# Softmax attention: the maximum subtracted on VectorE instead of GpSimd, two units interleaved

## What is computed

```python
qkv = xn @ Wqkv.T                      # q, k, v, 16 heads each
s = einsum('bhqd,bhkd->bhqk', q, k) * 16 ** -0.5
s = where(causal, s, -inf)
p = softmax(s, axis=-1)                # exp(s - max(s)) / sum
x = x + einsum('bhqk,bhkd->bhqd', p, v).reshape(b, t, 256) @ Wout.T + bout
```

## Time and profile before

| | |
|---|---|
| median of 3 runs | 2348.63 us (2345.78 to 2349.6) |
| the profiled execution: time | 2340.59 us |
| its span, first to last instruction | 2338.8 us |
| granted clock of TensorE, mean | 0.951 |
| busy: PE, PEld, DVE, ACT, POOL | 2115.2, 1578.8, 1472.2, 1112.8, 980.7 us |
| L1133, the subtractions on GpSimd | 64, 68.1 us busy, 1064 ns in the mean |

### The profile page before, as it was taken

The page is one execution under the profiler, slowest core; times in us unless marked ns, Lnnn a source line. Parts: engine busy times, 40 slices in busy tenths (PEclk is TensorE's granted clock), DMA queues, the critical chain, the costliest instruction groups (busy, mean ns, idle before and its releaser), DMA issues. The chain is left out here.

```text
span 2338.8 us, 57804 instructions
## 1 busy us (share of the span) xinstructions
PE 2115.2 (90%) x19590; PEld 1578.8 (68%) x19591; DVE 1472.2 (63%) x4145; ACT 1112.8 (48%) x2509; POOL 980.7 (42%) x1105
## 2 busy tenths in 40 slices
PE   6999999999989998999999999979969898777773
PEld 5888888888779986565566666647758787433331
DVE  5777777777656664784333333327867767777672
ACT  4666666666645442275122222216445555444542
POOL 4444444444300003344566666652123433145554
PEclk9999999999989988999899999989979999899996
DMA  4110010111000003040222222237710000000002
GB/s 137 33 31 30 30 30 30 30 30 30 30 8 10 11 10 111 1 198 18 77 87 85 88 87 85 87 124 279 240 42 11 7 9 7 3 0 1 0 0 72
DMA packets 120510, 128.80 MB, mean 55 GB/s; under 512 B 77537, under 2 KB 95074, under 8 KB 119138
## 3 DMA queue, kind: packets, MB, share of 16 engines
q1 hardware_dynamic: 104994, 87.12, 12.2%
q0 software_dynamic: 13824, 37.77, 5.1%
q10 hardware_dynamic: 1600, 2.72, 0.3%
HBM read 96.11 MB, written 27.26 MB: 53 GB/s over the span
## 5 line engine op out<-in xcount | busy, mean ns | idle before, releaser
L542 ACT ACTIVATE xa_prob<-xa_neg_s,xa_neg_max 128x256 f32<-128x256 f32 x512 | 224.5, 499 | 141.4 <-DVE xa_neg_max L420 141.4
L1904 PE MATMUL ex_ps_h<-moew_w,ex_xT 128*128 x576 | 274.9, 600 | 1.5 <-DVE ex_xT L1952 1.5
L1952 DVE COPY ex_xT<-ex_ps_x 128x256 f32<-128x256 f32 x144 | 61.1, 425 | 249.1 <-PE ex_ps_x L1911 249.1
L420 DVE CUSTOM_DVE_ANT_0 xa_neg_s<-xa_ps_s,xa_mask 128x256 f32<-128x256 f32 x512 | 191.4, 421 | 33.6 <-PE xa_ps_s L607 19.4
L1883 POOL DMA_INDIRECT ex_xg<-xn_rows,moe_in_row x144 | 139.6, 970 | 107.5 <-PE ex_ps_x L1911 98.6
L636 PEld LDWEIGHTS xa_ps_o<-xa_v,xa_probT 128*64 128x64 f32 x4096 | 141.2, 138 | 48.3 <-issue 43.0
L549 ACT ACTIVATE xa_probT<-xa_ps_s 128x512 f32<-128x512 f32 x256 | 152.0, 594 | 43.3 <-PE xa_ps_s L618 42.3
L636 PE MATMUL xa_ps_o<-xa_v,xa_probT 128*64 128x34 f32 x4096 | 170.2, 228 | 0.2 <-ACT xa_probT L549 0.2
L1937 ACT ACTIVATE ex_act_g<-ex_ps_h 128x256 f32<-128x256 f32 x144 | 55.2, 383 | 236.6 <-PE ex_ps_h L1904 236.6
L1888 POOL DMA_INDIRECT expert_outs<-moe_y,moe_out_row x144 | 142.1, 986 | 60.9 <-ACT moe_y L1941 59.1
L618 PE MATMUL xa_ps_s<-g_ident,xa_prob 128*128 128x128 f32 x1024 | 163.8, 283 | 2.7 <-ACT xa_prob L542 2.4
(11 more groups left out here) (319 smaller groups left out, 5090.1 us busy)
## 6 DMA issues: line engine op xcount, KB each, us to landing
xa_ctxT<-in_ctxT_dram SPq DMA_DIRECT2D x32, 512.0 KB, 3.6
xb_ctx_rows<-in_ctx_rows_dram SPq DMA_DIRECT2D x32, 512.0 KB, 3.7
xb_expert_y<-expert_outs SPq DMA_DIRECT2D x32, 512.0 KB, 4.4
moew_w<-in_moe_w_dram SPq DMA_DIRECT2D x8, 1024.0 KB, 11.8
xn_rows<-rs_xn SPq DMA_DIRECT2D x8, 512.0 KB, 2.9
moew_xw<-in_moe_w_dram SPq DMA_DIRECT2D x8, 512.0 KB, 19.7
out_dram<-g_x SPq DMA_DIRECT2D x1, 4096.0 KB, 13.5
g_x<-in_x_dram SPq DMA_DIRECT2D x2, 1536.0 KB, 15.3
```

What stands on the lines that cost most here:

```text
L420: ins = nc.vector.tensor_tensor_reduce(neg_s[:, u % 2, g, :], ps_s[j][:, g * S:(g + 1) * S], mask[:, b, :], -1.0, 3e38, ALU.add, ALU.min, ...
L542: ins = nc.scalar.activation(prob[:, u % 2, i, :], neg_s[:, u % 2, i, :], ACT.Exp, bias=neg_max[:, u % 2, i:i + 1], scale=-1.0)
L1904: mm = nc.tensor.matmul(ps_h[1 - par][:, :], xT[:, 1 - par, k, :], c.w1[:, own, k, :], start=(k == 0), stop=(k == KC - 1))
```

## The change

GpSimd no longer subtracts. VectorE does, in the same form (`less_largest`), and takes the units by twos in a new function, `below_maximum`: mask, maximum, mask of the next, subtract, maximum of the next, subtract of the next. What waited for GpSimd's subtraction before a unit's mask is now one wait ahead of each pair of units, on VectorE's own subtraction. The wait for the exponential two units back goes along with the subtraction. Sizes, buffers and the other engines' programs stay as they are.

```diff
--- before.py
+++ after.py
@@ -1126,13 +1126,6 @@
                 a = s - 2
                 if live(s, NP) and later(s):
                     start.inverse_std(pool, nc, s, par)
-                if live(a, NP):
-                    for j in range(4):
-                        pool.wait_ge(top_ready, 4 * a + j + 1)
-                        wait(pool, exp_ready, 4 * a + j - 1)
-                        nc.gpsimd.tensor_tensor(shifted[:, j % 2, :, :], masked[:, j % 2, :, :],
-                                                top[:, j % 2, :].unsqueeze(2).to_broadcast([P, 8, T]), ALU.subtract)\
-                            .then_inc(shift_ready, 1)
                 if live(s, NP):
                     pool.wait_ge(xn_ready, s + 1)
                     for i in range(2):
@@ -1143,14 +1136,32 @@
 
         @block.vector
         def _(dve):
-            def maximum(a, j):
+            def mask_added(a, j):
                 dve.wait_ge(s_done, 4 * a + j + 1)
-                wait(dve, shift_ready, 4 * a + j - 1)
                 nc.vector.tensor_tensor(masked[:, j % 2, :, :], ps_s[j][:, :].rearrange("p (n t) -> p n t", t=T),
                                         mask[:, :].unsqueeze(1).to_broadcast([P, 8, T]), ALU.add)\
                     .then_inc(masked_ready, 1)
+
+            def largest(a, j):
                 dve.wait_ge(masked_ready, 4 * a + j + 1)
                 nc.vector.tensor_reduce(top[:, j % 2, :], masked[:, j % 2, :, :], AX.X, ALU.max).then_inc(top_ready, 1)
+
+            def less_largest(a, j):
+                dve.wait_ge(top_ready, 4 * a + j + 1)
+                wait(dve, exp_ready, 4 * a + j - 1)
+                nc.vector.tensor_tensor(shifted[:, j % 2, :, :], masked[:, j % 2, :, :],
+                                        top[:, j % 2, :].unsqueeze(2).to_broadcast([P, 8, T]), ALU.subtract)\
+                    .then_inc(shift_ready, 1)
+
+            def below_maximum(a, j):
+                if j == 2:
+                    dve.wait_ge(shift_ready, 4 * a + 2)
+                mask_added(a, j)
+                largest(a, j)
+                mask_added(a, j + 1)
+                less_largest(a, j)
+                largest(a, j + 1)
+                less_largest(a, j + 1)
 
             def normalised_heads(e, i):
                 heads = ps_o[i][:, 0:H * D1].rearrange("p (h d) -> p h d", d=D1)
@@ -1188,15 +1199,14 @@
                                 k2[:, pp, 0, g, :, h2, :], ALU.mult, ALU.subtract)
                     ins.then_inc(k_ready, 1)
                 if live(a, NP):
-                    maximum(a, 0)
-                    maximum(a, 1)
+                    wait(dve, shift_ready, 4 * a)
+                    below_maximum(a, 0)
                 if live(e, NP):
                     dve.wait_ge(pv_done, 4 * e + 4)
                     for i in range(2):
                         normalised_heads(e, i)
                 if live(a, NP):
-                    maximum(a, 2)
-                    maximum(a, 3)
+                    below_maximum(a, 2)
                 if live(s, NP) and later(s):
                     wait(dve, xT_done, s - 1)
                     start.normalise(dve, nc, s, par)
```

## The result

The changed kernel took 2386.68 us in the median of 4 runs (2385.52 to 2391.67), against 2348.05 us (2345.78 to 2349.6) for the kernel before: a ratio of 1.0169, 95% interval 1.0154 to 1.0183. It is slower, as forecast, but by 38.6 us where the forecast had 26.2. Applied to the 2348.63 us from which the forecast started, the ratio gives 2388.3 us, just above the stated range, which ended at 2387. The profiled execution took 2387.38 us.

A forecast was written before the change was run, and what follows sets the result against it. The prediction took a circle of waits as the bound, with VectorE's run closing it. +2.40 and -0.73 us a step gave 21.7 us over thirteen steps, +26.2 with first and last ones: 2374.8 us, range 2366 to 2387.

The forecast's parts named there:

- VectorE's run as the side of the circle that sets the step: Softmax self-attention: VectorE's run from M, a step's first mask addition, to L1205's end grows from 8.58 to 10.25 us.
- +2.40 us for the subtractions: On VectorE, each of two pairs of units per step takes 3.84 us instead of 2.64, 1.20 more.
- -0.73 us for L233: VectorE's normalisation no longer meets GpSimd's last subtraction: 408 ns instead of 1137, in 14 steps.
- Rival 3: L233 stays slow for a reason other than GpSimd's last subtraction: 10.2 us missing, 2385.0 us; chance 0.10.
- The exponentials: First two come as before, TensorE's 1.22 us wait stays; a new wait for the third is hidden by L1205's lateness.
- First and last steps: First softmax step 1.8 us longer, next-to-last 2.1, last between 0 and 1.2, taken as 0.6.
- The sum: First step 1.8, thirteen steps 21.7, next-to-last 2.1 and last 0.6 us: together +26.2 us.
- Rival 4: Longer TensorE standstills lower its clock to 0.85 over the thirteen steps: 19 us more, 2394 us; chance 0.04.
- the forecast's own signs: Among them: TensorE's wait behind L1205 up from 0.65 to about 1.2 us, a new 0.4 for the third exponential.
- Rival 1: The chain through the subtraction to the first exponential sets the step: 22.4 us saved, 2326.2 us; chance 0.04.
- Rival 2: TensorE's own work absorbs the additional 1.67 us per step, no change: 2348.6 us; chance 0.03.

The follow-up runs named there:

- e3: The changed kernel with one idle 128x512 subtraction per step on GpSimd, started after VectorE's fourth subtraction so it lies over L233: 2417.77 us, 1.0289.
- e7: The kernel before with only the fourth unit's subtraction moved to VectorE, GpSimd keeping three: 2351.28 us, 1.0009.
- e1: The changed kernel with seven idle transposes of the identity on TensorE where it otherwise stands still before L1404: 2376.22 us, 1.0114.
- e6: The changed kernel without the interleaving: mask, maximum and subtraction of one unit, then of the next: 2411.28 us, 1.0258.
- e5: The changed kernel with the normalisation L233 ahead of the keys' remainder on VectorE: 2368.9 us, 1.0087.
- e4: The kernel before with three idle 128x512 maxima on VectorE ahead of L233, GpSimd keeping its subtractions: 2375.54 us, 1.0118.

## Why the prediction was right and wrong

- **VectorE's run as the side of the circle that sets the step**: right. Its end was forecast at M + 10.25 and lies at 10.26; the step was forecast at 18.44, and the clean one is 18.35.
- **+2.40 us for the subtractions**: right, 1.21 us a pair in the profile, at 688 ns each.
- **-0.73 us for L233**: right, and the cause was shown twice, by putting GpSimd on top again (e3) and by taking it away alone (e7). Rival 3 is refuted with it: no L233 takes over 410 ns in the changed kernel.
- **The exponentials**: right. The first keeps its wait (1.09 us), the third brings a new one (0.58).
- **First and last steps**: forecast 1.8 and 2.1 us. With the clock held up (e1), the first is 17.31 - 15.85 = 1.5 and the next-to-last 16.41 - 14.29 = 2.1. From the last M to the stage's last instruction it is 17.31 us instead of 16.76, 0.55 where 0.6 was taken.
- **The sum**: 26.2 us forecast; with the clock held up 27.0 by the medians and 24.4 + 0.55 = 25.0 by the steps.
- **The clock**: here the prediction failed. Rival 4 came in on top of the forecast, and I had given it 0.04 because "the single gaps stay at about 1.2 us, the length they have now, and the clock is full with those". That reason was wrong, and the forecast's own signs spoke against it: they had a longer wait before L1394 and a new one for the third exponential. In the kernel before, 1.22 us stand alone, and 0.65 us follow 4.6 us later. The change puts 0.58 and 1.25 us close behind each other, with 0.66 us of work between, and behind that the clock fell in seven of the thirteen full steps, in the first and in the last but one. It cost 14.3 us by the steps (10.5 by the medians against e1), which should have been a term of the sum. The 19 us that I had worked out for rival 4 came near by luck. They took a clock of 0.85 over the thirteen steps, where it was 0.95, and counted half of the loss, since half of a step is TensorE's run; with 0.95 the same sum gives some 6 us. The drops lay wholly in TensorE's run and so were paid in full, 1.48 us each.
- **Rival 1** (the chain through the subtraction): refuted by e6, where the first exponential comes earlier and the time rises. That VectorE subtracts in 0.69 us and GpSimd in 1.04 is right, and does not decide here, since VectorE has no time to spare.
- **Rival 2** (hidden): refuted. Every full step got longer by about 1.6 us or more; TensorE had no slack before L1404, where it waits in each.

Not settled: what it is in a standstill that brings the clock down. In the changed kernel it fell behind five of the seven standstills of 1.34 us and two of the six of 1.25 us before L1404, and the traces show no difference in TensorE's work ahead of them. Nor is it shown that it counts how close two standstills lie: in e5 0.57 and 0.60 us lie as close and the clock stayed full, and in e4 a single one of 1.70 to 1.78 us was followed by a drop in five steps of thirteen. No run here has two short ones of the same sum both close and apart.

## What to carry to other kernels

Before moving work to a faster engine, find the engine whose run closes the circle of waits, and charge the move to it; a shorter operation on the busier side is a loss. When a change lengthens TensorE's standstills, add the cost of its clock to the sum, and do not take a full clock with shorter ones as proof that it stays full. When one late wait is taken away, look for the next chain before pricing the gain: here the step fell by only 0.11 us.

## What was not expected of the hardware

Idle transposes on TensorE made a kernel faster: seven of them, 0.93 us per step, brought 10.5 us. A drop of the clock cost about 1.47 us in each full step that had one, in three kernels (19.83 against 18.35, 19.30 against 17.83, 20.42 against 18.94), and the longest standstill of TensorE ahead of one was 1.35, 1.78 and 2.07 us. And where GpSimd's 128x512 subtraction of SBUF tensors meets the two L233, the L233 that starts first keeps its 0.41 us, GpSimd loses 0.10 us, and the L233 that starts behind GpSimd ends with it: 1.14 us beside the subtraction of the kernel before, 1.36 beside that of e3.
